# The last of four gather passes in a graph network: rows picked by one-hot products; norm order in three projections

## The reference

```
x_src = x[src]
msg = where(rel == r, x_src @ weight[r] + bias[r])      # r = 0..3
agg = segment_max(msg, dst);  agg = 0 where no edge
h = x @ weight[-1] + bias[-1] + agg                     # out = x + h
```

## Time and profile before

| | |
|---|---|
| median of 3 runs | 5873.93 us (5870.14 to 5876.07) |
| the profiled execution | 5876.16 us, span 5874.4 us |
| busy: PE, PE weight load | 3278.1 us (56%), 2756.8 us (47%) |
| busy: DVE, ACT, POOL | 2906.4 (49%), 1827.9 (31%), 3903.4 (66%) |
| chain that ended last | POOL arena L557, 1%; the rest under 1% each |
| last pass, first to last gather | 4816.0 to 5793.4 us |

### The profile page before, as it was taken

How to read it: one execution, slowest core, us unless ns; L and a number is a source line. 1 busy time by engine, 2 the same in 40 slices (tenths; PEclk the granted TensorE clock), 3 DMA queues, 4 the chain that set the end, 5 groups by cost and what they waited for, 6 DMA issues and landing times. The chain is left out here.

```text
span 5874.4 us, 89970 instructions
## 1 busy us (share of the span) xinstructions
PE 3278.1 (56%) x15772; PEld 2756.8 (47%) x15773; DVE 2906.4 (49%) x7625; ACT 1827.9 (31%) x6493; POOL 3903.4 (66%) x4083
## 2 busy tenths in 40 slices
PE   3444555545555525889999894244555563334332
PEld 3444455444555523677777644233445533333331
DVE  4233344434455656788888852344555652222221
ACT  2111111111122213666666653233344441111110
POOL 4777777677777747777776003777777517777776
PEclk9667777766677756999999995566677785555555
DMA  4222222211111112344444211222222134444443
GB/s 122 61 62 63 63 65 66 72 53 52 53 53 52 53 41 78 111 113 117 119 117 113 95 46 31 52 53 54 53 53 52 38 111 130 133 132 130 131 133 107
DMA packets 441899, 474.71 MB, mean 81 GB/s; under 512 B 131954, under 2 KB 337214, under 8 KB 441695
## 3 DMA queue, kind: packets, MB, share of 16 engines
q0 software_dynamic: 130464, 264.37, 17.1%
q1 hardware_dynamic: 184116, 146.31, 8.3%
q10 hardware_dynamic: 127227, 63.09, 3.6%
HBM read 315.46 MB, written 157.97 MB: 81 GB/s over the span
## 5 line engine op out<-in xcount | busy, mean ns | idle before, releaser
L1194 PE MATMUL pa<-arena,weighted 128*128 x4480 | 860.0, 367 | 855.8 <-POOLq L913 511.2
L1194 PEld LDWEIGHTS pa<-arena,weighted 128*128 128x128 f32 x4480 | 795.4, 273 | 909.4 <-issue 909.2
L422 POOL DMA_INDIRECT arena<-y_tab,slot x784 | 739.8, 944 | 398.7 <-issue 209.4
L1607 POOL DMA_INDIRECT arena<-t_tab,src_idx x784 | 777.5, 992 | 265.7 <-issue 216.0
L919 POOL DMA_INDIRECT arena<-h_tab,src_idx x784 | 742.8, 947 | 308.1 <-issue 221.9
L2490 POOL DMA_INDIRECT arena<-t_tab,src_idx x784 | 753.3, 961 | 244.9 <-issue 224.6
L919 POOL DMA_INDIRECT arena<-sage_tab,src_idx x784 | 739.8, 944 | 262.4 <-issue 216.1
L471 DVE TENSOR_TENSOR_SCAN scan_t<-mask,scan_t,pa 128x512 f32<-128x512 bf16 x196 | 250.9, 1280 | 737.1 <-PE pa L495 737.1
L495 PE MATMUL pa<-ident,arena 128*128 128x128 f32 x784 | 218.3, 434 | 603.9 <-DMA arena<-y_tab,slot 603.9
L495 PEld LDWEIGHTS pa<-ident,arena 128*128 128x128 f32 x784 | 140.1, 217 | 681.9 <-DMA arena<-y_tab,slot 430.8
L2731 PE MATMUL pa<-weighted 128*128 128x130 f32 x2240 | 422.6, 364 | 21.0 <-ACT weighted L2809 11.0
(11 more groups left out here) (522 smaller groups left out, 6559.9 us busy)
## 6 DMA issues: line engine op xcount, KB each, us to landing
gat_tab<-out_rows SPq DMA_DIRECT2D x248, 260.0 KB
scan_rows<-out_rows ACTq DMA_DIRECT2D x196, 256.0 KB, 3.7
arena<-t_tab,src_idx POOLq DMA_INDIRECT x1568
mask<-cut_row SPq DMA_DIRECT2D x196, 128.0 KB, 3.1
arena<-h_tab,src_idx POOLq DMA_INDIRECT x784
arena<-sage_tab,src_idx POOLq DMA_INDIRECT x784
y_tab<-arena SPq DMA_DIRECT2D x49, 256.0 KB, 2.3
arena<-y_tab,slot POOLq DMA_INDIRECT x784, 2.8
```

The source lines that it names most:

```text
L422: nc.gpsimd.indirect_dma_start(out=rows(c, t), out_offset=None, in_=table[:, :], in_offset=bass.IndirectOffsetOnAxis(ap=slot[:, c, t:t + 1 ...
L1194: ins = nc.tensor.matmul(pa[:, b * CE:b * CE + RW], hot[b][:, t * P:(t + 1) * P], ring[:, bass.ds(start + t * RW, RW)], start=(t == 0), st ...
L1607: nc.gpsimd.indirect_dma_start(out=rows[:, g % QR * QT + t, :], out_offset=None, in_=t1_tab[:, :], in_offset=bass.IndirectOffsetOnAxis(ap= ...
```

## The change

The last pass now follows the walk of 160 steps, in groups of seven tiles, like the sage passes. Each step transposes its group, runs the scan over its 896 columns with the carry that belongs to it, transposes back, and multiplies with a one-hot that is 1 only at the last edge of each node of the block (edge numbers other than a last one are 0 in `last_rows`, written by SP and gathered by POOL in the opening of the block; the one-hots compare them with node numbers that lie in PSUM). The product is added to x; ACT stores the block before the current one at each step, and loads the mask of step i + 2 as soon as scan i is done. A group that meets two blocks is staged, transposed and scanned once for each. scan_rows, the 49 row-picking gathers and the final block are gone, with last_idx, slot and their set-up (two DVE steps and a transpose after the first sage pass, some memsets, a zero row). `same_block`'s counterpart for the carry is made of two flag rows (`on_flags`, `same_flags`).

In `project`, DVE runs front(i + 2) ahead of post(i) in all three projections; PE's turn(i + 1) and ACT's keep(i + 1) come before group i's tiles again, and wide products use two PSUM banks, so that a tile waits for the copy of the tile before last. group_col1 and block_col1 are buffers of their own for the four-head pass, so that the last pass finds group_col and block_col as sage left them.

The diff, cut to its core. `project`:

```diff
                         front(dve, 1)
 
                     def step(i, b, left):
-                        if left > 1 and starts is None:
+                        if left > 1:
                             front(dve, i + 2)
                         dve.wait_ge(group_product.sem, group_product.past(i + 1))
                         post(dve, i, b)
-                        if left > 1 and starts is not None:
-                            front(dve, i + 2)
 
...
                             if by_tile is not None:
-                                if t == 4 and left > 0:
-                                    turn(i + 1)
                                 ws, bias, n, _ = by_tile
 
-                                pe.wait_ge(tile_out.sem, tile_out.by_last_lap(i * NG + (max(t, 1) if t < 3 else max(t - 1, 2))))
-                                to = banks[t % 4][:, 0:n]
+                                pe.wait_ge(tile_out.sem, tile_out.by_last_lap(i * NG + (t + 1 if t > 1 else 2 - t)))
+                                to = pb[:, t % 2 * CE:t % 2 * CE + n]
...
                     def step(i, b, left):
-                        if left > 0 and by_tile is None:
+                        if left > 0:
                             turn(i + 1)
-                        multiply(i, b, left)
+                        multiply(i, b)
...
                     def step(i, b, left):
-                        if left > 0 and by_tile is None:
+                        if left > 0:
                             keep(i + 1, 1 - b)
                         if by_tile is not None:
                             for t in range(NG):
-                                if t == 4 and left > 0:
-                                    keep(i + 1, 1 - b)
                                 if t == NG - 2 and left > 1:
                                     scalar_front(act, i + 2)
```

The last pass (the lines of `edge_pass` and of the final block that it replaces stand in the kernel above):

```diff
-        edge_pass(y_tab, D, y_idx, cut_row, ALU.add, ALU.max)
...
+                for g in range(GN):
+                    if g >= RG:
+                        pool.wait_ge(group_freed.sem, group_freed.past(g - RG + 1))
+                    for t in range(GT):
+                        nc.gpsimd.indirect_dma_start(
+                            out=edge_rows[:, g % RG * GT + t, 0:D], out_offset=None, in_=y_tab[:, :],
+                            in_offset=bass.IndirectOffsetOnAxis(ap=y_idx[:, g * GT + t:g * GT + t + 1], axis=0)
+                        ).then_inc(group_gathered[g % RG].sem, 16)
+                    if g == LAP:
+                        pool.wait_ge(stored.sem, stored.past(16))
+                        for k in range(2):
+                            nc.gpsimd.indirect_dma_start(out=rel_rows[k], out_offset=None, in_=last_rows[:, :],
+                                                         in_offset=bass.IndirectOffsetOnAxis(ap=group_col[:, k:k + 1], axis=0)
+                                                         ).then_inc(table_rows.sem, 16)
+                    if g > 0:
+                        landed(g - 1)
+                landed(GN - 1)
...
+                sp.dma_start(dst_again, dst_rows[:, :]).then_inc(lasts_here.sem, 16)
+                sp.wait_ge(ends_ready.sem, ends_ready.past(1))
+                sp.dma_start(last_rows[:, :], lasts).then_inc(stored.sem, 16)
+                with sp.Fori(0, GN) as g:
+                    n = sp.value_load(retire_walk[0:1, bass.ds(g, 1)], min_val=1, max_val=SN)
+                    wait_apart(sp, edge_staged.sem, edge_staged.past(n))
+                    sp.sem_inc(group_freed.sem, 1)
+                sp.wait_ge(block_added.sem, block_added.past(SN))
+                sp.dma_start(out[(NT - 1) * P:N, :], x[0:NL, NT - 1, :]).then_inc(stored.sem, 16)
+                sp.wait_ge(stored.sem, stored.past(32))
...
+                def scan(s, b):
+                    after(dve, edge_turned, s + 1)
+                    after(dve, mask_loaded[b], (s - b) * 8 + 16)
+                    after(dve, edge_back, s - 1)
+                    after(dve, carry_ready, s)
+                    v.tensor_tensor_scan(run_t[b], mask_t[b], turned_ps[b], carry_t[b], ALU.add, ALU.max).then_inc(edge_scanned.sem, 1)
+                def carry_on(s, b):
+                    after(dve, edge_scanned, s + 1)
+                    v.tensor_scalar(held_at, run_t[b][:, GE - 1:GE], of_step(on_flags, s + 1), None, ALU.mult).then_inc(carry_held.sem, 1)
+                    after(dve, carry_held, s + 1)
+                    v.scalar_tensor_tensor(out=carry_t[1 - b], in0=carry_t[b], scalar=of_step(same_flags, s + 1), in1=held_at,
+                                           op0=ALU.mult, op1=ALU.add).then_inc(carry_ready.sem, 1)
+                def build(s, b):
+                    after(dve, block_summed, s - 1)
+                    at = rel[:, s * GT:(s + 1) * GT] if isinstance(s, int) else rel[:, bass.ds(s * GT, GT)]
+                    v.tensor_tensor(hot[b].rearrange("p (t n) -> p t n", n=P),
+                                    node_row.unsqueeze(1).broadcast_to([P, GT, P]),
+                                    at.unsqueeze(2).broadcast_to([P, GT, P]), ALU.is_equal).then_inc(hot_built.sem, 1)
+                def add(s, b):
+                    j = block_of(dve, s, b)
+                    row = x[:, bass.ds(j, 1), :].rearrange("p j d -> p (j d)")
+                    after(dve, block_summed, s + 1)
+                    after(dve, block_added, s)
+                    after(dve, block_stored, (s - 2) * 16)
+                    v.tensor_tensor(row, row, last_ps, ALU.add).then_inc(block_added.sem, 1)
+                def body(i, b):
+                    if inside(i):
+                        scan(i, b)
+                    if inside(i - 2):
+                        add(i - 2, b)
+                    if inside(i):
+                        carry_on(i, b)
+                        build(i, b)
+                tables()
+                relative()
+                walk_steps(dve, body)
...
+                def turn(s, b):
+                    after(pe, edge_staged, s + 1)
+                    after(pe, edge_scanned, s - 1)
+                    for t in range(GT):
+                        ins = nc.tensor.transpose(turned_ps[b][:, t * P:(t + 1) * P], staged_t[b][:, t * P:(t + 1) * P], ident[:, :])
+                    ins.then_inc(edge_turned.sem, 1)
+                def back(s, b):
+                    after(pe, edge_scanned, s + 1)
+                    after(pe, edge_kept, s)
+                    for t in range(GT):
+                        ins = nc.tensor.transpose(back_ps[:, t * P:(t + 1) * P], run_t[b][:, t * P:(t + 1) * P], ident[:, :])
+                    ins.then_inc(edge_back.sem, 1)
+                def select(s, b):
+                    after(pe, edge_kept, s + 1)
+                    after(pe, hot_built, s + 1)
+                    after(pe, block_added, s)
+                    for t in range(GT):
+                        ins = nc.tensor.matmul(last_ps, hot[b][:, t * P:(t + 1) * P], kept_t[b][:, t * P:(t + 1) * P],
+                                               start=(t == 0), stop=(t == GT - 1))
+                    ins.then_inc(block_summed.sem, 1)
+                def body(i, b):
+                    if inside(i + 1):
+                        turn(i + 1, 1 - b)
+                    if inside(i - 1):
+                        select(i - 1, 1 - b)
+                    if inside(i):
+                        back(i, b)
+                tables()
+                relative()
+                walk_steps(pe, body)
...
+                def stage_group(s, b, start, need):
+                    after(act, edge_turned, s - 1)
+                    wait_apart(act, group_landed.sem, group_landed.past(need))
+                    nc.scalar.copy(staged_t[b].rearrange("p (t d) -> p t d", d=D),
+                                   ring[:, bass.ds(start, GT * RW)].rearrange("p (t w) -> p t w", w=RW)[:, :, 0:D]
+                                   ).then_inc(edge_staged.sem, 1)
+                def load_mask(s, b, need):
+                    after(act, edge_scanned, s - 1)
+                    act.dma_start(mask_t[b], cut_row[0:1, bass.ds((need - 1) * GE, GE)].broadcast_to([P, GE])).then_inc(mask_loaded[b].sem, 16)
+                def keep_back(s, b):
+                    after(act, edge_back, s + 1)
+                    after(act, block_summed, s - 1)
+                    nc.scalar.copy(kept_t[b], back_ps).then_inc(edge_kept.sem, 1)
+                def store(s, j):
+                    after(act, block_added, s)
+                    after(act, block_stored, s * 16)
+                    act.dma_start(out[bass.ds(j * P, P), :], x[:, bass.ds(j, 1), :].rearrange("p j d -> p (j d)")
+                                  ).then_inc(block_stored.sem, 16)
+                STEP = [(0, NT - 2), (0, (RG - 1) * GT * RW), (1, GN)]
+                def body(i, b):
+                    if not isinstance(i, int) or 0 <= i < SN + 2:
```

(53 more changed lines are left out.)

292 lines of the change are left out of this document (100 added, 192 removed).

## The result

The changed kernel takes **5940.4 us** (median of four, 5937.0 to 5941.1) against 5872.0 (four, 5870.0 to 5876.1): ratio 1.0114, interval 1.0097 to 1.0132. The forecast was 5938. The profiled execution took 5941.1 us, its span 5939.3, which is 64.9 over the span of before.

| stretch | before | after | difference | forecast |
|---|---|---|---|---|
| start to the first transpose of sage's projection | 2086.5 | 2083.4 | −3.1 | −1 |
| from there to the end of the first scatter | 91.6 | 82.5 | −9.1 | −13 |
| to the first transpose of the second projection | 1380.3 | 1382.9 | +2.6 | 0 |
| from there to the end of its scatter | 99.3 | 80.4 | −18.9 | −16 |
| to the first transpose of the third | 1058.7 | 1056.9 | −1.8 | 0 |

A forecast was written before the change was run, and what follows sets the result against it. The last pass was taken as bound by POOL's gathers, then by late steps after the change. 5876 + 92 (last pass) − 13 − 16 (projections) − 1 (set-up) = 5938 us; likeliest case 5890 to 5975, 8 in 10 over all 5825 to 6020.

The forecast's parts named there:

- The chain of a step: Last pass: PE's three parts, then two ACT copies in series; 3.4 + 2.1 = 5.5 us at full clock, 8.5 at half.
- The cycle: Last pass: 6.8 us a step, with PE's clock falling and coming back; bursts starting slow 7.2, staying fast 5.5.
- The end of the pass: Steps fall behind the gathers at 319 us; the last pass takes 1150 us from the first gather against 1058, +92.
- Rival 1: Last pass: PE's clock stays up, cycle 5.5 us, pass −34, program 5812 us; chance 0.21.
- the other cycles in that list: Last-pass times for other step cycles: 6.3 gives 1091 us, 7.0 1170, 7.5 1235, 8.5 1385.
- Rival 2: Last pass: ACT's gap is 2.8 us, the store's DMA issue not hidden; cycle about 7.5, program 6023 us; chance 0.12.
- Sage's projection: First projection: fronts run in DVE's idle time, scatters end at 2164.6 in place of 2178.1, −13 us.
- I leave the pitch at 1.287: Sage's projection: POOL's scatters stay 1.287 us apart although DVE is now busy while POOL writes descriptors.
- the 13 us by which I had priced it: Sage's projection: if DVE contention made each scatter take 1.24 us, 49 × 0.26 = 13 us would go again.
- The second projection: Projection w2: early fronts bring groups to 10.0 us on ACT, scatter ends at about 3641.6 against 3657.7, −16 us.
- The two added edits: Projections: turn before multiply and two banks for four; said to act in the second, two banks costing nothing.
- The third: Projection w3: fronts were first already, a later first tile is offset by steadier groups; 0, between −7 and +7 us.

The follow-up runs named there:

- kept_twice_2: The changed kernel with ACT's copy of the finished block made twice, timed again after a first measurement with a slow reference: 5948.6 us, ratio 1.0121 to the kernel before.
- pe_filled: The changed kernel with ten further transposes on PE after each back(i), filling its wait: 5811.2 us, ratio 0.9897 to the kernel before.
- fronts_alone: The kernel before with only DVE's front(i + 2) ahead of post(i) in the projections that start a scatter: 5847.9 us, ratio 0.9959.

## Why the prediction held, and where it did not

- **The chain of a step: right, term by term.** PE waits 2.08 to 2.12 us (forecast 2.1) for ACT's copy in, which took 0.937 (0.94), behind a copy back of 0.906. The full-clock cycle is 5.40 (5.5). Two orders that break the chain show it as the cause.
- **The cycle: 6.82 against 6.8, partly luck.** I mixed bursts of 7.2, 5.5 and 6.5 to 7, leaning on the sage pass. The long ones are 7.05, most of them start at full clock and fall on their way, and they outnumber the short ones by six to one. kept_twice_2 shows how little I knew of this: the same way of thinking gave 7.6 to 7.9 there, and 6.83 came.
- **The end of the pass: right.** First step 42.5 us after the first gather (forecast 40), +95.3 against +92; the cost appears as POOL's waits for freed groups, as forecast, and as 102 us of steps behind the last gather.
- **Rival 1** named the right time for its condition (pe_filled), but the clock does not stay up by itself. The time was in part luck: worked out as the one for 6.8 is, with 12 us to fill and 15 to drain, a cycle of 5.5 gives a pass of 1029 us and not 1024 (the other cycles in that list are 2 to 5 us low too), and the program 5817. The Trainium skill (TensorE: Matmul & The Clock Gate, "HAM oscillation") blames idle stretches of a DMA's length. The trace disagrees in that shorter ones do it too: 2.1 us of idle time in 5.4 cost 1.4 us a step. **Rival 2** falls: the store's issue lies under the copy.
- **Sage's projection: −9.1 against −13, a term mis-sized.** The first post came 2.3 us later, as forecast (2.2). The failed step is "I leave the pitch at 1.287". The 49 scatters took 67.5 us where 63 were counted. POOL's rows, then DVE's beside them:

```profile
2104.84 1.82 POOL L428 DMA_INDIRECT start_rows<-nodeval,start_idx  x1 [0.30 <-issue]
2106.97 0.98 POOL L428 DMA_INDIRECT start_rows<-nodeval,start_idx  x1 [0.30 <-issue]
2112.17 1.82 POOL L428 DMA_INDIRECT start_rows<-nodeval,start_idx  x1 [0.30 <-issue]
2118.16 1.03 POOL L428 DMA_INDIRECT start_rows<-nodeval,start_idx  x1 [0.30 <-issue]
```

```profile
2104.73 1.08 DVE L1282 TENSOR_TENSOR x<-arena,stat  x1
2112.06 1.08 DVE L1282 TENSOR_TENSOR x<-arena,stat  x1
2117.24 1.09 DVE L625 SCALAR_TENSOR_TENSOR h<-arena,moments 128x896 f32 x1 [0.21 <-DVE moments L621]
```

  DVE's operation ends at 2105.81, 2113.14 and 2118.33, the scatter that began inside it at 2106.66, 2113.99 and 2119.19: each time 0.85 to 0.86 us later. A scatter that begins while DVE works on two SBUF operands ends no sooner than 0.85 us after that operation; the one at 2106.97, outside any, took 0.98. The row of before on which I rested (POOL at 2103.40) began 0.03 us before the end of one such operation and 0.48 us ahead of the next, so it could not show this. And my reading that only the first scatter of a group is long was wrong in that trace already, where the fifth of a group took 1.77:

```profile
2153.70 1.08 DVE L825 SCALAR_TENSOR_TENSOR weighted<-arena,moments 128x896 f32<-128x896 f32 x1
2153.87 1.77 POOL L620 DMA_INDIRECT start_rows<-nodeval,start_idx  x1 [0.30 <-issue]
```

  That it takes two SBUF operands, and not just a long DVE operation, is seen on POOL's gathers in the trace of the changed kernel. First a scan of two SBUF operands in the four-head pass, then one of the last pass, which reads its data from PSUM:

```profile
2191.99 2.02 DVE L1511 TENSOR_TENSOR_SCAN arena<-keep,weighted 112x896 f32<-112x896 f32 x1
2192.94 1.81 POOL L1395 DMA_INDIRECT arena<-t_tab,src_idx  x1 [0.30 <-issue]
```

```profile
5503.40 2.08 DVE L2771 TENSOR_TENSOR_SCAN weighted<-mask,alpha,pb 128x896 f32<-128x896 bf16 x1 [1.77 <-PE pb L2828]
5503.47 0.94 POOL L2699 DMA_INDIRECT arena<-y_tab,y_idx  x1 [0.30 <-issue]
```

  The 273 gathers of the last pass that began more than 0.3 us before the end of such a scan or of the one-hot (L2783, which reads the node numbers from PSUM) took 0.940 to 0.953 us; the eight in the scans L1511 and L1528 took 1.67 to 2.40.

  The Trainium skill's rule (SBUF — State Buffer, "Who interferes with whom") that I had set aside has the two contend, with the order of issue deciding who waits. The trace agrees for the scatter, which waits where it comes second; a DVE operation that begins 0.08 us or more into a scatter takes no longer for it (1.08 to 1.09 us with and without). The delays cost far less than the 13 us by which I had priced it: over their usual 0.982 the 49 scatters have 4.7 to 4.8 us in all in every run with fronts first, and 2.2 before.
- **The second projection: −18.9 against −16**, inside its bounds: POOL stands 0.3 to 0.9 us between groups, where before it stood 4.9 to 5.5 between most. The two added edits that I reasoned through at length did nothing (fronts_alone). **The third: 0, as forecast.** The set-up gave 3.1 in this pair where I had 1. The six usual traces of the changed kernel and its variants reach that point at 2083.4 to 2086.4 (mean 2084.9), the three with the old set-up at 2085.8 to 2087.3 (mean 2086.5): 1.6 us less on average, with ranges that overlap, so about half of the 3.1 may be spread between runs.
- The errors nearly cancel, to +3 in all, which is luck: +4 and −3 in the projections, −2 in the set-up, +3 in the pass, +1 in the stretches between.

## What to carry to other kernels

Where every engine has time to spare and the kernel is still late, follow one step around the engines: a copy that stands in program order behind a wait for the last work of the step before makes the whole a serial chain, and moving it ahead of that wait was worth 153 us here. When a cost in such a chain is changed, read both the gap and the clock after it, since the clock can hide or double the change: a total that stays the same does not show that the cost was off the path. Before using a row as proof that two engines do not disturb one another, look at which of the two began first.

## What the runs showed of the hardware

- The granted clock does not follow the idle time alone. At equal work of PE (28 instructions a step) it was 0.78 with 2.1 us idle in 5.4, 0.88 with 2.7 in 6.0, and 0.97 with 1.7 to 1.9 in 5.0 to 5.2. Which rhythm decides was not tried further and stays open.
- A scatter of POOL's that begins inside a DVE operation with two SBUF operands ends no sooner than 0.85 us after it, and so takes up to 1.86 us in place of 0.98. Gathers do the same (0.75 us after a scan, up to 2.40 in place of 0.94), and do not where one of DVE's operands lies in PSUM.
